# The gathers of edge rows without a bound on their row numbers, in the second and the last stage of a graph network

## The reference

```python
n = layernorm(x)                                   # layer 1: graph
x = x + segment_sum(w[:, None] * (n @ Wl)[dst], src) + bl + n @ Wr + br
n = layernorm(x)                                   # layer 2: 8 dense experts
x = x + sum_e softmax(mean(n) @ Wr + br)_e * (relu(bn(relu(bn(n @ W1[e])) @ W2[e])) @ Wo[e] + bo[e])
n = layernorm(x)                                   # layer 3: graph
x = x + segment_sum(w[:, None] * (n @ W)[src], dst) + bias
n = layernorm(x)                                   # layer 4: one of 32 experts per node
x = x + relu(relu(n @ W1[i] + b1[i]) @ W2[i] + b2[i])   # i = argmax(n @ router.T + b)
```

## Time and profile before

| | |
|---|---|
| median of 3 runs | 3277.88 us (3269.11 to 3279.42) |
| the profiled execution | span 3279.4 us, time 3279.42 us |
| mean granted TensorE clock | 0.904 of full |
| TensorE (PE) busy | 2782.1 us, 85% |
| VectorE (DVE) / ScalarE (ACT) / GpSimd (POOL) busy | 64% / 62% / 62% |
| rows gathered by POOL's queue | 207.48 MB in 87808 packets, 22.3% of 16 DMA engines |

### The profile page before, as it was taken

One profiled execution on the slowest core, in us unless ns is written; L12 is line 12 of the kernel. 1 busy time (PEld: TensorE's weight loads), 2 busy tenths in 40 slices (PEclk: granted clock), 3 DMA queues, 4 the chain that ended last, 5 costly groups with the idle time before them and its releaser, 6 DMA issues. The chain is left out here.

```text
span 3279.4 us, 51092 instructions
## 1 busy us (share of the span) xinstructions
PE 2782.1 (85%) x17781; PEld 2480.7 (76%) x17781; DVE 2084.8 (64%) x3782; ACT 2041.7 (62%) x4125; POOL 2023.7 (62%) x1692
## 2 busy tenths in 40 slices
PE   6899837799999999999999944788888988888889
PEld 6789726688888888888888834677777777777778
DVE  8689654577676777677766535556555655656652
ACT  4377456687888788777876525545455555555551
POOL 0355467676677677776773028776677777766750
PEclk9999957799999999999999975689898998989989
DMA  2133452223233323232331023233333333323320
GB/s 67 5 85 74 111 165 87 73 89 94 84 92 94 94 86 96 87 95 84 91 95 58 14 82 114 87 96 92 94 89 97 97 103 97 94 85 92 99 74 14
DMA packets 159242, 280.89 MB, mean 86 GB/s; under 512 B 42474, under 2 KB 107778, under 8 KB 158722
## 3 DMA queue, kind: packets, MB, share of 16 engines
q0 software_dynamic: 87808, 207.48, 22.3%
q1 hardware_dynamic: 70884, 68.48, 6.7%
q10 hardware_dynamic: 288, 1.61, 0.1%
HBM read 240.67 MB, written 36.77 MB: 85 GB/s over the span
## 5 line engine op out<-in xcount | busy, mean ns | idle before, releaser
L1310 POOL DMA_INDIRECT f_got<-h_tab,list_cols x784 | 952.8, 1215 | 390.1 <-issue 235.9
L1953 POOL DMA_INDIRECT n_got<-h_tab,edge_cols x784 | 894.4, 1141 | 333.9 <-issue 226.9
L2069 PE MATMUL bank<-n_mhi,n_hot 128*128 128x256 f32 x1168 | 339.1, 318 | 155.6 <-DMA n_got<-h_tab,edge_cols 99.3
L2016 ACT ACTIVATE n_hrh<-bank 128x512 fp32r<-128x512 f32 (+1 forms) x208 | 118.9, 572 | 560.4 <-remote 275.9
L1580 DVE TENSOR_TENSOR f_hlo<-edge_cols,f_hhi 128x1024 fp32r<-128x1024 f32 (+1 forms) x208 | 241.6, 1161 | 331.9 <-ACT f_hhi L1389 266.8
L1384 ACT ACTIVATE edge_cols<-bank,f_shf,f_scl 128x512 f32<-128x512 f32 (+1 forms) x416 | 296.3, 745 | 169.3 <-PE bank L1301 114.8
L1466 PE MATMUL bank<-f_mhi,f_hot 128*128 128x256 f32 x1168 | 330.7, 314 | 64.9 <-DVE f_mlo L1574 55.6
L2069 PEld LDWEIGHTS bank<-n_mhi,n_hot 128*128 128x128 f32 x1168 | 246.0, 211 | 184.2 <-DMA n_got<-h_tab,edge_cols 108.8
L1997 ACT ACTIVATE n_got<-n_got,edge_cols 128x256 f32<-128x256 f32 x784 | 333.1, 500 | 79.1 <-DMA n_got<-h_tab,edge_cols 78.8
L1362 ACT ACTIVATE f_got<-f_got,list_cols 128x256 f32<-128x256 f32 x784 | 332.5, 496 | 44.3 <-DMA f_got<-h_tab,list_cols 44.1
L2070 PE MATMUL bank<-n_mlo,n_hot 128*128 128x256 f32 x1168 | 324.0, 305 | 28.5 <-issue 28.2
(11 more groups left out here) (318 smaller groups left out, 7599.5 us busy)
## 6 DMA issues: line engine op xcount, KB each, us to landing
f_got<-h_tab,list_cols POOLq DMA_INDIRECT x784
n_got<-h_tab,edge_cols POOLq DMA_INDIRECT x784
n_rows<-acc_tab SPq DMA_DIRECT2D x12, 512.0 KB
out_rows<-n_rows SPq DMA_DIRECT2D x12, 512.0 KB
edge_cols<-in_w SPq DMA_DIRECT2D x16, 256.0 KB
acc<-in_x SPq DMA_DIRECT2D x4, 896.0 KB, 7.2
h_tab<-hbuf SPq DMA_DIRECT2D x7, 512.0 KB
acc_tab<-base SPq DMA_DIRECT2D x7, 512.0 KB
```

The lines of the kernel that those rows point to most:

```text
L1310: nc.gpsimd.indirect_dma_start(got[:, s % RING0, u, :], None, h_tab[0], bass.IndirectOffsetOnAxis(gidx0[:, s * U + u:s * U + u + 1], 0), b ...
L1953: nc.gpsimd.indirect_dma_start(got[:, s % RING, u, :], None, h_tab[1], bass.IndirectOffsetOnAxis(gidx[:, s * U + u:s * U + u + 1], 0), bou ...
L2069: nc.tensor.matmul(tile_bank(t), lhs, mhi[:, s % 3, u, :], start=begins, stop=False)
```

## The change

The argument `bounds_check=ROWS - 1`, with `oob_is_err=True`, is left off the gathers of stage 2 and of stage 3. `ROWS - 1` is 6271. Without it the row numbers are taken as they are. The row numbers, the tables, the rings, the semaphores and the order of issue are unchanged. The scatters of stage 1 had no bound and have none; the code that is skipped keeps its bounds.

```diff
@@ -1309,8 +1309,7 @@
                     for u in range(U):
                         nc.gpsimd.indirect_dma_start(
                             got[:, s % RING0, u, :], None, h_tab[0],
-                            bass.IndirectOffsetOnAxis(gidx0[:, s * U + u:s * U + u + 1], 0),
-                            bounds_check=ROWS - 1, oob_is_err=True).then_inc(s_got[s % RING0], 16)
+                            bass.IndirectOffsetOnAxis(gidx0[:, s * U + u:s * U + u + 1], 0)).then_inc(s_got[s % RING0], 16)
@@ -1952,8 +1951,7 @@
                     for u in range(U):
                         nc.gpsimd.indirect_dma_start(
                             got[:, s % RING, u, :], None, h_tab[1],
-                            bass.IndirectOffsetOnAxis(gidx[:, s * U + u:s * U + u + 1], 0),
-                            bounds_check=ROWS - 1, oob_is_err=True).then_inc(s_got[s % RING], 16)
+                            bass.IndirectOffsetOnAxis(gidx[:, s * U + u:s * U + u + 1], 0)).then_inc(s_got[s % RING], 16)
```

## The result

| | before | after |
|---|---|---|
| median of 4 runs beside each other | 3278.65 us (3269.11 to 3280.2) | 3326.68 us (3316.49 to 3342.14) |
| ratio after to before | | 1.0152 (95% interval 1.0116 to 1.0187) |
| the profiled execution: span, clock | 3279.4 us, 0.904 | 3314.8 us, 0.900 |

The kernel became 1.5% slower. The forecast was 3274 us with a range of 3240 to 3290, so it was wrong, and on the wrong side.

A forecast was written before the change was run, and what follows sets the result against it. TensorE was taken to bound stage 2 but for its ramp and later stage 3, POOL the ramp of stage 3. 3279.4 less 4.2 us for the MOVEs gave 3275.2, for the median 3274 us, range 3240 to 3290.

The forecast's parts named there:

- Step (a): Gathers of stages 2 and 3: the register write before each, a MOVE of 29 ns, goes, saving 4.2 us.
- Step (b): Gathers of stages 2 and 3: the compare of 128 row numbers goes, taken as zero; minimum stays 1006 ns.
- Rival 1: Gathers: the check is real work, at 100 ns each; 3247 to 3260 us, say 3256; chance 0.36.
- Step (c): Gathers of stages 2 and 3: time over the 1.006 us minimum, 164 and 106 us, stays, from meeting VectorE's subtractions.
- Step (d): Transfers, semaphores, rings and order of issue stay, so no wait is added; no term in the sum.
- rival 3: Gathers on POOL: the form without a bound is dearer, at 519 ns more 3830 us; chance 0.13.

The follow-up runs named there:

- e6: Kernel after with the bound put back on two gathers of each four; 3318.06 us against 3311.36 for the kernel before, ratio 1.0018.
- e3: Kernel before without the bounds, an unused MOVE kept before each gather in both stages; 3113.29 us against 3156.45, ratio 0.9859.
- e10: The kernel of e3 run again at another time; 3114.71 us, ratio 0.9865 to the kernel before.
- e15: The kernel of e3 run a third time; 3111.13 us, ratio 0.9851 to the kernel before.
- e2: Kernel before with the bound left off in stage 3 alone; 3119.13 us against 3156.45, ratio 0.9878.
- e11: The kernel of e2 run again at another time; 3122.76 us, ratio 0.9885 to the kernel before.
- e16: The kernel of e2 run a third time; 3120.37 us, ratio 0.9879 to the kernel before.
- e4: Kernel after with an empty instruction on POOL before each gather in both stages; 3115.45 us against 3156.45 for the kernel before, ratio 0.9865.
- e7: Kernel after with 64 MB of unused memory ahead of the tables; 3362.39 us against 3311.36 for the kernel before, ratio 1.0142.
- e8: Kernel before with 64 MB of unused memory ahead of the tables; 3304.68 us against 3311.36, ratio 0.9977.
- e5: Kernel after, unchanged, run again; 3358.56 us against 3311.36 for the kernel before, ratio 1.0121.
- e1: Kernel before with the bound left off in stage 2 alone; 3153.45 us against 3156.45, ratio 0.9991.
- e9: Kernel after with a one-byte memset on POOL before each gather; 3113.56 us against 3157.88 for the kernel before, ratio 0.9853.
- e13: Kernel after with two one-byte memsets on POOL before each gather; 3112.74 us against 3156.90 for the kernel before, ratio 0.9865.

## Why the prediction was wrong

- **Where the bound is.** The windows and the chain of waits said that TensorE holds stage 2 and the middle of stage 3 and POOL the ramp. For the kernel of the comparison that holds: its chain after the ramp is TensorE's. On chip A POOL holds all of stage 3. One set of runs could not show that the kernel is near the border of the two.
- **Step (a), the MOVEs.** The gap stayed 0.30 us, as forecast. That the MOVE carries the bound is shown by e6, which has 392 of them for 392 bounds in stage 3. The 4.2 us are worth nothing on chip A: with the MOVEs kept stage 3 takes 1188.7 to 1195.4 us (e3, e10, e15), without them 1193.1 to 1195.5 (e2, e11, e16).
- **Step (b), the compare.** It was put at zero and is 66 ns a gather, 0.5 ns a row. That alone crosses the 50 ns at which the forecast called itself wrong. The argument that a minimum and a median 6 ns apart are fixed work was right, but the compare is part of the fixed work. Rival 1 had the mechanism, at 100 ns. By its own terms 66 ns would have given 13 to 22 us (138 x 0.066 + 4.2 at the low end, two thirds of the other's 26.6 and 4.2 at the high one); chip A gives 41 to 46 (e3, e4, e10, e15), since there all 784 gathers of stage 3 count.
- **Step (c), the excess.** The means exceed the minima by 0.207 and 0.130 us (before 0.209 and 0.135). This step was right. Counted in the traces, of the gathers that take over 100 ns more than the shortest, all but one run beside a TENSOR_TENSOR of VectorE: 416 of 417 in the two stages before, 392 of 392 after. The gathers beside none have a mean of 1012 to 1015 ns before and 945 to 946 after. So the excess belongs to VectorE's instructions, which the change doesn't touch. The rule of the Trainium skill ("SBUF — State Buffer", section "Who interferes with whom"), that a VectorE instruction with two inputs in SBUF contends with a GpSimd instruction that reads SBUF, agrees with that. The same section of the Trainium skill infers that descriptor generation is not held up by such an instruction; for these gathers the measurement says otherwise.
- **Step (d), nothing is added.** True of the instructions, and the step that misled. From "no wait is added and the gather is not longer" I took it that the kernel cannot lose except by a dearer gather (rival 3, which did not happen). But TensorE stood 124 us of stage 3 in "issue" (the earlier trace rows have 52.1 of them), in bursts that no wait explains. I took this for constant and put its change at nothing without a reason. It grew by 57 us; the landings (15 less) and the rest (15 less) gave back 30, and 27 were lost.
- **The rivals.** None foresaw a loss with a shorter gather, and the chance of slower, 0.13, was all in rival 3. The right rival would have been: TensorE's idle time by issue, 124 us, is not a constant of the program.

**What stays open.** Why the bursts lengthen when gathers are shorter. What was tried: the place of the tables is not it (e7, e8), and with half of the bounds, a quarter of the saving on POOL, the median has a seventh of the loss (e6). The bursts have no fixed place in the program: with stage 3 cut into blocks of 50 products, the idle time by issue in the kernel after and in e5, the same program, correlates at 0.12, while e1 and e2 of chip A have theirs at the same products (0.76). What was not tried where it happens: a kept MOVE, a padding, or the change in one stage; all of these fell on chip A, where the bursts are absent. So the pace of the gathers, the missing MOVEs in the instruction stream and the place of the code are still all possible. Open also is what makes the bursts come on chip B and in the comparison and not on A. The larger packets of the instruction queues are 144 in each kernel, 53 of them in stage 3, and take the same mean there (1.05 to 1.12 us in before, after, e1, e2 and e5), so neither more nor slower fetches are it. Nor do they lie beside the pauses: of the 222 gaps of the kernel after, 35 have a packet of an instruction queue in them or in the 3 us before, fewer than the 65 that the same gaps have on average when shifted by 2.5 to 40 us.

No version beats the kernel before in both places. Where POOL is the bound, the change brings 1.4 to 1.5% (the kernel after itself did not run there; e3, e4, e9, e10, e13 and e15 carry only padding that takes no time in stage 3); where the bursts are, it costs 1.2 to 1.5%.

## What to carry to other kernels

Before a faster engine is called harmless, add up the bounding engine's idle time by "issue": where it is large (here 124 of 1332 us) and comes in bursts without waits, it can move by more than the edit is worth (here by 57 us, upwards), and deserves a chance of its own. A gain that depends on which of two engines bounds a stage should be measured on more than one chip, as the same edit here gave 0.985 to 0.987 (with free padding) and 1.012 to 1.015. To learn whether an engine paces a stage, pad it and shorten it: if the stage follows count times cadence both ways, it does.

## What the runs showed of the hardware

- The bound of an indirect gather of 128 rows costs POOL 66 ns in each, 1006 to 940 ns. Where two of four have it (e6), those with it take 1027 ns in the median and those without 967, so in a mixture both are 15 to 21 ns longer than alone (1012 and 946).
- A gather runs long when it meets VectorE: of the 392 gathers of the kernel after that exceed the shortest by over 100 ns, all lie beside a TENSOR_TENSOR.
- Between two gathers lie 0.30 us into which a MOVE, an empty instruction or one or two one-byte memsets go free; an iota of 0.20 us makes the idle and padding time 0.36 to 0.37 us and the cadence 0.08 to 0.09 us longer (1.25 to 1.33 and 1.31 to 1.40).
- One unchanged kernel took 3156 us on one chip (3144 to 3166, 17 runs) and 3311 us on another (3291 to 3333, 23 runs). What the traces differ in is TensorE's pauses without a wait and the time at its lower clock that follows them (346 us in stage 3 of the comparison's kernel before, 374 in e8, 206 in e1); whether that is the whole of it is not shown.
